# Scales folded into the k rows, the turned rows' low parts ahead of the inversion, and Pool's first weight folds behind the first negated rows

## The reference

```python
x = L0_attn_x                                   # (2, 4096, 256)
xn = _layernorm(x, axis=-1)
x = x + attention(xn, W_qkv, b_qkv) + ffn(xn, ...)
# attention: 16 heads of 16 columns, no factor on the scores
qkv = (xn @ W_qkv + b_qkv).reshape(B, D, 3, H, p).transpose(2, 0, 3, 1, 4)
scores = softmax(einsum('bhip,bhjp->bhij', q, k), axis=-1)
out = einsum('bhij,bhjp->bhip', scores, v)
# ffn: h = xn @ W_exp + b_exp; butterfly of 10 stages; + up_bias; exact gelu; butterfly; @ W_con + b_con; + down_bias
```

## Time and profile before

| | |
|---|---|
| median of 3 runs | 5333.88 us |
| the profiled execution, own time | 5331.87 us |
| its span, first to last instruction | 5330.1 us |
| granted PE clock, mean | 0.994 |
| busy: PE, ACT, DVE, POOL | 99%, 93%, 90%, 29% |

### The profile page before, as it was taken

One profiled execution on the slowest core, in us unless ns is written; L12 is line 12 of the kernel. 1 busy time (PEld: TensorE's weight loads), 2 busy tenths in 40 slices (PEclk: granted clock), 3 DMA queues, 4 the chain that ended last, 5 costly groups with the idle time before them and its releaser, 6 DMA issues.

```text
span 5330.1 us, 98874 instructions
## 1 busy us (share of the span) xinstructions
PE 5278.1 (99%) x36138; PEld 2262.5 (42%) x36138; DVE 4805.7 (90%) x9106; ACT 4953.3 (93%) x9745; POOL 1572.1 (29%) x677
## 2 busy tenths in 40 slices
PE   8999999999999999999999999999999999999999
PEld 7433333333333333333333333333333333333798
DVE  7899999999999999999999999999999999997333
ACT  6799999999999999999999999999999999999544
POOL 2668885122221222212222212221122221221000
PEclk9899999999999999999999999999999999999999
DMA  7410111000000000000000000000000000000111
GB/s 238 155 29 36 44 52 29 13 10 13 13 13 11 6 13 13 13 13 10 13 13 13 13 6 11 13 13 13 13 10 13 13 13 11 6 13 10 36 47 35
DMA packets 212355, 140.01 MB, mean 26 GB/s; under 512 B 149288, under 2 KB 189096, under 8 KB 209320
## 3 DMA queue, kind: packets, MB, share of 16 engines
q1 hardware_dynamic: 208432, 110.90, 8.0%
q0 software_dynamic: 3456, 23.07, 1.2%
HBM read 88.75 MB, written 42.99 MB: 25 GB/s over the span
## 4 chain that ended last, share of the span: by engine, by line
PE 45%; ACT 33%; DVE 11%; issue 7%; DVEq 0%; ACTq 0%
ACT probs L884 27%; PE psum L1174 16%; PE psum L1136 14%; PE psum L1160 8%; DVE maxima L957 7%; ACT spill L900 5%; PE psum L1277 3%; PE psum L1262 3%; DVE merged L953 2%; PE psum L1115 1%; DVE o_t L1001 1%; DVE neg_parts L982 0%; DVE neg_parts L986 0%; DVE neg_max L973 0%; DVE maxima L953 0%
## 5 line engine op out<-in xcount | busy, mean ns | idle before, releaser
L884 ACT ACTIVATE probs<-psum 128x512 f32<-128x512 f32 x8192 | 4268.3, 627 | 93.2 <-PE psum L1160 61.2
L957 DVE TENSOR_REDUCE maxima<-psum 128x1 f32<-128x512 f32 x6042 | 3871.7, 684 | 163.4 <-PE psum L1136 118.6
L1160 PE MATMUL psum<-q_rows,k_rows 50*128 50x512 f32 x8192 | 2337.5, 482 | 0.0
L1136 PE MATMUL psum<-k_halves,q_halves 48*128 48x512 f16 x7049 | 2199.4, 386 | 14.9 <-DVE maxima L957 5.0
L1174 PE MATMUL psum<-probs,v_cols 128*17 128x512 f32 x16384 | 2161.0, 599 | 3.7
L1160 PEld LDWEIGHTS psum<-q_rows,k_rows 50*128 50x128 f32 x8192 | 1300.5, 187 | 153.9 <-ACT probs L884 71.7
L1136 PEld LDWEIGHTS psum<-k_halves,q_halves 48*128 48x128 f16 x7049 | 530.0, 93 | 1404.8 <-DVE maxima L953 823.1
L785 POOL TENSOR_TENSOR o_t<-o_t,recip 128x256 f32<-128x256 f32 x64 | 39.7, 621 | 3208.2 <-DVE recip L1005 3208.2
L708 POOL TENSOR_SCALAR q_rows<-q_halves,unscales 48x2048 fp32r<-48x2048 f16 x128 | 696.4, 5441 | 12.1
L953 DVE CUSTOM_DVE_ANT_0 merged<-psum,spill 128x512 bf16<-128x512 f32 x1007 | 690.2, 685 | 9.4 <-PE psum L1136 7.1
L900 ACT ACTIVATE spill<-psum 128x512 f32<-128x512 f32 x1007 | 629.1, 625 | 11.9 <-PE psum L1136 6.4
(11 more groups left out here) (131 smaller groups left out, 2376.6 us busy)
## 6 DMA issues: line engine op xcount, KB each, us to landing
q_halves<-q_parts SPq DMA_DIRECT2D x384, 64.0 KB, 2.2
k_halves<-k_parts SPq DMA_DIRECT2D x192, 64.0 KB, 2.3
planes<-in_up_planes POOLq DMA_DIRECT2D x10, 1024.0 KB, 5.0
planes<-in_down_planes POOLq DMA_DIRECT2D x10, 1024.0 KB, 5.0
y<-in_x SPq DMA_DIRECT2D x16, 512.0 KB, 4.3
xn_transposed<-xnt SPq DMA_DIRECT2D x16, 512.0 KB, 5.2
q_parts<-parts SPq DMA_DIRECT2D x32, 256.0 KB, 5.7
k_parts<-parts SPq DMA_DIRECT2D x32, 256.0 KB, 2.9
```

Of the source, the lines that this page charges most:

```text
L884: nc.scalar.activation(probs[:, 2 * (u % 2) + half, BANK * g:BANK * g + BANK], ps_s[:, r % 4, :], ACT.Exp).then_inc(s_exp, 1)
L957: nc.vector.tensor_reduce(largest, region(use), axis=AX_X, op=ALU.max).then_inc(s_region_free, 1)
L1136: nc.tensor.matmul(region(use_of[n, j]), q_halves[lower:lower + ROWS, m % 2, P * t:P * t + P], keys[lower:lower + ROWS, :], start=True, st ...
L1160: nc.tensor.matmul(ps_s[:, r % 4, :], k_rows[s // 2 % 2][lower:lower + ROWS + MAX_PARTS, key:key + P], q_rows[s % 2][lower:lower + ROWS + ...
```

## The change

It has five parts. The expansion of q becomes one plain copy over 114 partitions (`EXPANDED`) in place of two multiplications over 48; the expansion of k becomes one multiplication over 114 partitions, by the product of q's and k's unscale (`max_scale`). For that POOL presets `q_halves` with zeros and `k_halves` with ones at the kernel's start; the rows between the halves and the rows of ones then come with the copy, and the four transfers of ones, their memset and the waits on them go. The maxima are no longer unscaled: `high_part` is a copy and `low_part` a subtraction. In the preparation ACT takes the root ahead of banks 2 and 3, and DVE does `low_turned` before `scale_mean`. ACT computes one element's exponential at the start of the second part of the program. POOL's folds of block 0 wait for the first negated rows, and `place_neg` waits for the expansion of its block.

```diff
@@ -259,6 +262,8 @@
                 pool.wait_ge(s_ident, IDENT)
+                nc.gpsimd.memset(q_halves[:, :, :], 0.0).then_inc(s_preset, 1)
+                nc.gpsimd.memset(k_halves[:, :, :], 1.0).then_inc(s_preset, 1)
                 pool.wait_ge(s_w, 16 * 5)
@@ -307,6 +312,7 @@
                         sp.wait_ge(s_diff_out, 16 * KD)
+                        sp.wait_ge(s_preset, 2)
@@ -355,6 +361,8 @@
                         if m == KD and left > 1:
                             copy_turned(c + 1, 1 - p)
+                        if m == KD and left > 2:
+                            deviation(c + 2, p)
                         act.wait_ge(s_qk_ps, 2 * KD * c + m + 1)
@@ -363,7 +371,6 @@
                     if left > 2:
-                        deviation(c + 2, p)
                         normalise(c + 2, p)
@@ -464,10 +471,10 @@
                         low_part(c, m)
+                    if left > 1:
+                        low_turned(c + 1, 1 - p)
                     if left > 2:
                         scale_mean(c + 2, p)
-                    if left > 1:
-                        low_turned(c + 1, 1 - p)
@@ -696,33 +701,25 @@
-                    for lower in (0, HALF_P):
-                        rows = slice(lower, lower + ROWS)
-                        q_chain(nc.gpsimd.tensor_scalar(q_rows[m % 2][rows, :], q_halves[rows, m % 2, :],
-                                                        unscales[rows, head:head + 1], None, ALU.mult))
+                    nc.gpsimd.tensor_copy(q_rows[m % 2][0:EXPANDED, :], q_halves[0:EXPANDED, m % 2, :]).then_inc(s_qx, 1)
...
-                    for lower in (0, HALF_P):
-                        rows = slice(lower, lower + ROWS)
-                        k_chain(nc.gpsimd.tensor_scalar(k_rows[n % 2][rows, :], k_halves[rows, n % 2, :],
-                                                        unscales[rows, head:head + 1], None, ALU.mult))
+                    nc.gpsimd.tensor_scalar(k_rows[n % 2][0:EXPANDED, :], k_halves[0:EXPANDED, n % 2, :],
+                                            max_scale[0:EXPANDED, head:head + 1], None, ALU.mult).then_inc(s_kx, 1)
...
-                nc.gpsimd.memset(probs[0:MAX_PARTS, 2, :], 1.0).then_inc(s_ones, 1)
@@ -794,6 +791,8 @@
                         expand_q(s + 1)
+                    if s == 0:
+                        pool.wait_ge(s_neg_in, 2 * 16)
                     for k in range(WEIGHT_OPS * s, min(WEIGHT_OPS * s + WEIGHT_OPS, 6 * len(rows_of_turns))):
                         fold_weights(k)
@@ -811,17 +810,13 @@
                     sp.wait_ge(s_region_free, vector_uses[use_of["neg", m]])
+                    sp.wait_ge(s_qx, m + 1)
...
-                sp.wait_ge(s_ones, 1)
-                for slot in range(2):
-                    for lower in (0, HALF_P):
-                        dst = k_rows[slot][lower + ROWS:lower + ROWS + MAX_PARTS, :].bitcast(F32)
-                        sp.dma_start(dst, probs[0:MAX_PARTS, 2, :]).then_inc(s_ones_in, 16)
@@ -899,12 +893,12 @@
+                nc.scalar.activation(warm[0:1, 1:2], one[0:1, 0:1], ACT.Exp)
                 for n in range(PAIRED):
                     for i in range(PAIRS_OF_TILE):
                         rectify_pair(n, i)
                 for n in range(PAIRED, AHEAD):
                     rectify(n)
-                act.wait_ge(s_ones_in, 16 * 4)
@@ -973,18 +967,13 @@
-                    nc.vector.tensor_scalar(neg_parts[:, 0:QT], neg_max[:, :], unscale(m), None, ALU.mult).then_inc(s_fin, 1)
+                    nc.vector.tensor_copy(neg_parts[:, 0:QT], neg_max[:, :]).then_inc(s_fin, 1)
...
-                    nc.vector.scalar_tensor_tensor(neg_parts[:, QT:2 * QT], neg_max[:, :], unscale(m), neg_parts[:, 0:QT],
-                                                   ALU.mult, ALU.subtract).then_inc(s_fin, 1)
+                    nc.vector.tensor_tensor(neg_parts[:, QT:2 * QT], neg_max[:, :], neg_parts[:, 0:QT], ALU.subtract).then_inc(s_fin, 1)
```

More of the change, by code:

```diff
@@ L75, in attention_and_butterfly_ffn @@
     MAX_PARTS = 2
+    EXPANDED = P // 2 + ROWS + MAX_PARTS
     HALF_N = N // 2
@@ L191, in attention_and_butterfly_ffn @@
         s_minus = sem("minus_k_made")
+        s_preset = sem("q_and_k_halves_preset")
         s_ident = sem("ident_made")
@@ L698, in _ @@
             def _(pool):
-                q_chain, k_chain = Chain(pool, s_qx), Chain(pool, s_kx)
                 def expand_q(m):
@@ L704, in expand_q @@
                     pool.wait_ge(s_q[m % 2], 16 * LOADS * (m // 2 + 1))
-                    head = m // 2 % HEADS
-                    for lower in (0, HALF_P):
-                        rows = slice(lower, lower + ROWS)
-                        q_chain(nc.gpsimd.tensor_scalar(q_rows[m % 2][rows, :], q_halves[rows, m % 2, :],
-                                                        unscales[rows, head:head + 1], None, ALU.mult))
+                    nc.gpsimd.tensor_copy(q_rows[m % 2][0:EXPANDED, :], q_halves[0:EXPANDED, m % 2, :]).then_inc(s_qx, 1)
                 def expand_k(n):
@@ L714, in expand_k @@
                     pool.wait_ge(s_k[n % 2], 16 * K_LOADS * (n // 2 + 1))
-                    head = HEADS + n % HEADS
-                    for lower in (0, HALF_P):
-                        rows = slice(lower, lower + ROWS)
-                        k_chain(nc.gpsimd.tensor_scalar(k_rows[n % 2][rows, :], k_halves[rows, n % 2, :],
-                                                        unscales[rows, head:head + 1], None, ALU.mult))
+                    head = n % HEADS
+                    nc.gpsimd.tensor_scalar(k_rows[n % 2][0:EXPANDED, :], k_halves[0:EXPANDED, n % 2, :],
+                                            max_scale[0:EXPANDED, head:head + 1], None, ALU.mult).then_inc(s_kx, 1)
                 expand_k(0)
@@ L832, in _ @@
                     if more:
-                        sp.wait_ge(s_qx, 2 * (s + 1))
+                        sp.wait_ge(s_qx, s + 1)
                         load_q(sp, head, s % 2, s % 2)
                     if more and s % 2 == 0:
-                        sp.wait_ge(s_kx, 2 * head)
+                        sp.wait_ge(s_kx, head)
                         load_k(sp, head, head % 2)
@@ L845, in _ @@
                 sp.wait_ge(s_neg_in, 2 * 16 * SUPER)
-                sp.wait_ge(s_ones_in, 16 * 4)
                 for n in range(2):
@@ L1010, in split_w_up @@
                         dve.wait_ge(s_score, 2 * QG * LAST)
-                        dve.wait_ge(s_qx, 2 * SUPER)
-                        dve.wait_ge(s_kx, SUPER)
+                        dve.wait_ge(s_qx, SUPER)
+                        dve.wait_ge(s_kx, SUPER // 2)
                     nc.vector.tensor_copy(w_up_high[:, k, :], w_up[:, k, :]).then_inc(s_wu_high, 1)
@@ L1153, in score @@
                     if u % UNITS == 0 and r == 0:
-                        pe.wait_ge(s_qx, 2 * (s + 1))
-                        pe.wait_ge(s_kx, 2 * (s // 2 + 1))
+                        pe.wait_ge(s_qx, s + 1)
+                        pe.wait_ge(s_kx, s // 2 + 1)
                         pe.wait_ge(s_neg_in, 2 * 16 * (s + 1))
```

6 lines of the change are left out of this document (removed).

## The result

Before 5333.88 us, after **5299.12 us** (median of 4 runs, 5298.66 to 5300.3): ratio 0.9935, 95% interval 0.9918 to 0.9952, 34.8 us less. The forecast was 5317.3 us with a range of 5311 to 5326. The profiled execution after took 5298.86 us, with a span of 5297.1.

What follows compares the result with a forecast made beforehand. It took ACT to bound blocks without folds and a DVE-POOL collision to cost those with folds. -13.7 - 0.5 - 1.0 - 1.4 = -16.6 us from 5331.87 gave 5315.3, put at 5317.3 us for the median; range 5311 to 5326.

Steps and rivals of the forecast that it cites:

- What bounds the kernel now: Attention blocks: ACT bounds those without folds, DVE close behind; 14.5 us lost in eight blocks with folds, mostly by collision.
- The collision: Blocks with folds: `high_part` and `low_part` no longer meet POOL's last folds, -13.7 us, with 0.8 kept for grazing.
- `low_part` at the first scores: Before the first scores: first folds wait, so `low_part` takes 0.2 us instead of 0.69 beside a fold, -0.5 us.
- the table load: ACT's 1.28 us load at the first scores moves to the second part's start, where ACT is idle: -1.0 us.
- The preparation: Projection chunks: of two late starts on `xt_low`, 0.83 and 1.08 us, the second goes and part of the first: -1.4 us.
- The rest: POOL's presets at the start, dropped transfers of ones and their waits, new wait of `place_neg`: taken as 0.
- the slow copy: Rival: POOL's copy for q is as slow as the multiplication, 5.44 us, giving 5321.6 us; chance 0.24.
- partitions: Rival: POOL's time grows with partitions, 12.9 us for an instruction over 114, giving 5335.1 us; chance 0.04.
- the presets: Rival: POOL's presets hold DVE's products at the kernel's start, +3.5 us, giving 5320.8 us; chance 0.07.
- the collision was what cost: Against the rival that PE's clock or the folds' transfers cost the time in blocks with folds, 5331.0 us; chance 0.10.
- the eight blocks from the second negation: Sign of being right: these blocks, with folds on POOL, take about 590 us.
- the parts: Sign of being right: `high_part` and `low_part` near 0.23 us in all blocks, at most two of them longer.

Runs made afterwards that it cites:

- b_shift: Kernel before with one more one-element Relu ACTIVATE in ACT's program, ahead of the attention part's first Relu: 5321.34 us, 0.9981.
- a_nowarm: Kernel after without the early one-element exponential, so ACT's stream stands one place back: 5306.32 us, 0.9956 of the kernel before.
- b_dve: Kernel before with `high_part` and `low_part` as copy and subtraction without a factor, POOL multiplying by 1.0: 5329.45 us, 0.9998.
- a_dve: Kernel after with `high_part` and `low_part` in the old form, by a column of ones, plus a wait on DVE: 5303.26 us, 0.9948 of before.
- a_slow: Kernel after with POOL's expansions of q and k as long as before, each in two multiplications: 5314.9 us, 0.9965 of the kernel before.
- a_fold: Kernel after without the wait of POOL's first folds for the first negated rows: 5303.49 us, 0.9946 of the kernel before.

## Why the forecast was wrong

It had the mechanism of its main term right and left a second one of the same size out.

- *The step that failed: "What bounds the kernel now", and with it the zero for every block without folds.* I read 73.47 and 73.76 us as "the two parities of a head's blocks", took ACT as the bound and DVE (71.0) as standing "close behind it", and priced the new `high_part` and `low_part` only where they collided, at 0.23 us each as before. The 0.29 us between the parities were a hold of ACT (b_shift -6.9 us in the 52 blocks, a_nowarm +7.9), and at the block's end DVE was the last (b_dve -5.3, a_dve +5.1). Together 12.2 to 13.0 of the 12.9 us measured there. The four kernels agree on it: 3830.7 us with both, 3823.8 without the hold, 3825.5 and 3825.7 without the old form (b_dve and a_nowarm), 3817.8 with neither. Half of this could be read in the profile of before, where the chain of work that ended last runs over DVE at the end of every one of these blocks. The other half hung on the number of instructions ahead, which no cost of an instruction tells.
- *The collision, -13.7:* right in mechanism, too small in size. Measured -16.7, undone by a_slow at +16.6. I compared with blocks of 589.46 us, which lost 2.0 us of their own (587.4 after), and kept 0.8 for a grazing that didn't come: the copy took 1.89 us, the lower bound, and not 2.6. It went with 0.4 us to spare, and with the 2.6 us of the forecast it would have grazed.
- *`low_part` at the first scores, -0.5, and the table load, -1.0:* together -0.5 measured, up to the second negation. The table load shows nothing there (a_nowarm), where a difference below 1.6 us can't be told from chance. The folds' wait is worth about 6 us (a_fold), but against a kernel that never was: it mends what the shorter expansions would have done. Its reason, two transfers at once, was in none of my steps.
- *The preparation, -1.4:* measured -2.9, and -3.2 alone. I counted the two gaps above 0.8 us; the four chunks behind them were late in smaller pieces as well (9.35 to 9.66 us from chunk to chunk, for 9.24), and all but 0.06 us of it went.
- *The rest, 0:* held. The weights landed 0.9 us later in the profiled execution, and in executions of either kernel at any time from 10.3 to 12.2 us.
- *The rivals:* the slow copy fell (1.89 us), partitions cost nothing (5.45 us on 114 for 5.44 on 48), the presets held nobody, and the collision was what cost. Of the signs named, the eight blocks from the second negation came at 587 for 590, and the parts at 0.165 for 0.23 us. The Trainium skill's rule of "SBUF — State Buffer", section "Who interferes with whom", that a copy can take the pair of ports that DVE shares with GpSimd, and that an operation with two SBUF inputs contends with GpSimd's reads, agrees with the traces: beside POOL's folds the copy took up to 2.25 us (b_dve) and 2.42 (a_slow), the subtraction 0.84 (a_slow), for 0.165 each alone. The roughly line rate of one-input work in "GPSIMD Engine Reference", section "Engine selection", fits the copy (0.92 ns an element) and still not the multiplication (2.66).

## What to carry to other kernels

Where blocks of equal work differ in length by a constant few tenths of a microsecond, find out which instruction is late before taking it as the nature of the block: a change that adds or drops one instruction will move it. Price an edit of a few hundredths of a microsecond by its engine's place at the end of the block and by how often it comes, and expect the price to end once another engine is last. And when work on one engine gets shorter, look at what it issues next and whose transfer that meets.

## What the hardware showed that I had not expected

- ACT and DVE are each held for about 0.3 us at one place in 128 instructions of their own program, where the instruction there is on the path. ACT's hold was moved at will (1, 64 and 128 places; 0.26 to 0.30 us a block where it meets the path), DVE's by 4 and, by the way, by 1 (a_dve). It costs only where it meets an instruction on the path: ACT passes place 63 three times in two blocks and loses time at one; whether it is held at the other two can't be seen. What the engine does in it is open. The page of the kernel after counts 195 packets of 8.2 KB in a queue of instructions, and the four engines other than PE left 25,973 records, 133 for each packet; in the kernel before one such packet begins 0.3 us behind ACT's place 63 at 1673.4 us and one 0.9 us behind that at 1723.0. Between 900 and 4800 us of that trace such a packet begins within 1.5 us behind 53 of the 79 instructions of ACT at place 63, and behind 6 at most at any place outside 56 to 67. That fits a refill of 128 instructions, but no run here took the refill away.
- POOL copies 114 x 2048 f16 elements to fp32r in 1.89 us and multiplies the same by a column in 5.44; by the constant 1.0 it took 5.36 (a_slow). On 16 elements it takes 0.20 us, where DVE takes 0.16.
- DVE's 16-element operations take 0.225 us with a pointer to a factor and 0.165 without, 0.06 each, and DVE's next instruction starts that much earlier.
